# Layer 1 attention: GpSimd's moments between its last fetches, and ScalarE's four normalisations at the end of an iteration

## The chip, the core and the metric

The kernel runs on one core of one Trainium2 chip. The metric is the device time of one execution, in microseconds; the median of the runs shown is compared. TensorE (PE) multiplies and transposes, VectorE (DVE) and ScalarE (ACT) work elementwise, GpSimd (POOL) computes moments and issues the indirect transfers, SyncE (SP) issues the plain ones. Each engine runs its own program in the order in which it is written, and semaphores tie them together.

## The reference, cut to what matters

128 sequences of 64 tokens with 128 channels go through two layers. Each layer is a gated cross attention on a layernorm of x, and then a gated mixture of eight experts. The change lies in the second layer's attention (one head, causal) and in the first steps of its router.

```python
x = x + tanh(g_xattn[0]) * L0_xattn(layernorm(x), ctx, ctx)   # 16 heads
x = x + tanh(g_ffn[0])   * L0_ffn(layernorm(x))               # top 2 of 8 experts
x = x + tanh(g_xattn[1]) * L1_xattn(layernorm(x), ctx, ctx)   # 1 head, causal
x = x + tanh(g_ffn[1])   * L1_ffn(layernorm(x))               # each expert takes its 17 best tokens of a sequence

# L1_ffn
scores = softmax(einsum('bsd,ed->bse', x, router_w))
gate_vals, sel_idx = top_k(swapaxes(scores, 1, 2), 17)
tokens = x[b_idx, sel_idx]
y = gelu(tokens @ w1 + b1) @ w2 + b2
out = zeros_like(x).at[b_idx, sel_idx].add(y * gate_vals)
```

Every layernorm needs mean and variance of each token's 128 channels. Every token's row is in a tile of 128 tokens, so there are 64 tiles, in 16 groups of four.

## The kernel before, in words

Four stages follow each other: layer 0 attention (to about 337 us of the profiled span), layer 0's experts, layer 1 attention (about 584 to 684 us), and layer 1's experts. The stages overlap a little at their edges. No scheduler takes part: each engine's order is that of the Python loops in `scalar_program`, `tensor_program`, `vector_program`, `gpsimd_program` and `sync_program`, and tables of numbers at the top say in which iteration a side task is done.

**Layer 1 attention** is a loop over u from -2 to 16 that all engines write out with the same index. In iteration u:

- PE transposes the normalised tokens of group u+2 (`turn_tokens1`, L640), multiplies the keys' folded projection of group u+2 (`project1`, L936) and the values of group u+1 (`values1`, L943), transposes the shifted scores of group u (`turn1`, L967), computes the scores of group u+1 (L954, L958) and the output of group u (`output1`, L980).
- ACT copies the transposed tokens of group u+2 out of PSUM (L1723), normalises two tiles of group u+3 (`norm1`, L1880), copies the projection (`projected1`, L1900), computes the exponentials of group u (L1910) and normalises the other two tiles of group u+3.
- DVE finds the largest score of group u (L1536), subtracts it (L1540), adds the attention's output of group u-1 to x (L1551, L1554), copies the values of group u+1 with their bias (L1546), and then does side work: `combine(t)` adds layer 0's expert results of a late tile t (two instructions, L1451), `statistics1` and `statistics_router1` take a group's sums (L1124) before its layernorm and before the router.

**From iteration 7 on** (`ROUTE1_FROM`) the router's first call, `route1(0)`, is threaded through the loop. Each engine makes three steps of it in an iteration. Its steps on PE are the transposes of x (L777) and the logits (L809) of groups 0 to 3, on ACT the copies of both (L1723, L1921). DVE waits through eight steps and in the ninth, at the end of iteration 9, multiplies the logits by the inverse standard deviations (L1571). That step waits for the semaphores `s_lg1` (ACT's four copies of logits) and `s_mom2` (GpSimd's moments of 16 tiles). After it come the softmax, a transpose (L1016), and the choice of the 17 best tokens (L1583 to L1586, L1592 to L1595), which ends in iteration 11.

**GpSimd** fetches layer 0's expert results of tiles 48 to 63 in this stage (`get`, two indirect transfers a tile, L2100). A fetch waits until DVE has combined the tile six before it, since six buffers go round. `moments` turns sums into the mean times the inverse deviation and the inverse deviation (eleven or ten small instructions, L2006 to L2018; the power is L2014) for eight tiles. `moments1` serves the attention's `norm1`, `moments_router1` the router.

**SP** stores each finished group of x (L609) and, after the store of group `SPREAD_AT`, spreads the chosen tokens' lists (L587 to L604). DVE's `pick1` of tiles 0 to 3 (L1613, L1127), in iterations 14 and 15, waits for them. `LATER_BY` says how many of the last 16 tiles are combined by the end of iteration u: iteration 7 combines tiles 59 and 60, iteration 8 tiles 61 and 62, iteration 9 tile 63.

After the loop PE gathers the chosen tokens (L1031), ACT copies them (L1941), and the experts of layer 1 begin (L1067, L1077), with GpSimd adding their results to the output (L2182).

Of the kernel before, what the change touches and what calls it, by code (L numbers as in the profile page):

```python
# [23 lines left out]
TG = 4  # L24
NG = NT // TG
# [9 lines left out]
TS = 8  # L35
NSG = NT // TS
NS = 16
# [7 lines left out]
PARTS = ((0, 24), (24, 24), (48, 16))  # L45
# [70 lines left out]
COUNT_AT, SOFTMAX_AT, GATES_AT = 11, 12, 18  # L116


SPREAD_AT = 11
PICKED = {14: (0, 1), 15: (2, 3)}  # L120

LATER_BY = (0, 1, 3, 5, 7, 9, 11, 13, 15, 16)


def later_by(u):
    return LATER_BY[max(0, min(u, len(LATER_BY) - 1))]

# [88 lines left out]
def build(nc, t_in, out):  # L216
    with ExitStack() as ctx:
# [3 lines left out]
        def sem(name):  # L221
            return ctx.enter_context(nc.semaphore(name))
# [154 lines left out]
        def vec(name, n=1):  # L377
# [54 lines left out]
        s_st3, s_mom2, s_ltr1, s_lnTr1, s_lgm1, s_lg1 = [sem(n) for n in (  # L432
            "s_st3", "s_mom2", "s_ltr1", "s_lnTr1", "s_lgm1", "s_lg1")]
# [31 lines left out]
        def sync_program(e):  # L465
# [141 lines left out]
            for g in range(NG):  # L607
                w.wait_ge(s_x3, TG * g + TG)
                e.dma_start(out[:, TG * g:TG * g + TG, :], x_sb[:, TG * g:TG * g + TG, :]).then_inc(s_out, 16)  # L609
                if g == SPREAD_AT:  # L610
                    spread_lists(0)
# [1092 lines left out]
        def scalar_program(e):  # L1704
# [170 lines left out]
            def norm1(g, tiles):  # L1875
                w.wait_ge(s_mom1, g // 2 + 1)
                w.wait_ge(s_lt1, g - 1)
                for t in tiles:
                    n = TG * g + t
                    ins = e.activation(ln_sb[:, g % 2, t, :], x_sb[:, n, :], ACT.Identity, bias=nmr[:, n:n + 1], scale=rstd[:, n:n + 1])  # L1880
                if t == TG - 1:
                    ins.then_inc(s_ln1, 1)
# [13 lines left out]
            def projected1(g):  # L1896
                w.wait_ge(s_sc1, g - 1)
                w.wait_ge(s_g1, g + 1)
                w.wait_ge(s_yb, NBL - NW + 1)
                e.activation(g1[:, g % 2, :], banks[7], ACT.Identity, bias=fold1[:, 3:4]).then_inc(s_ge1, 1)  # L1900

            def tokens1(g):
                w.wait_ge(s_sc1, g - 1)
                w.wait_ge(s_q, NG)
                copy_turned(g % 2, 6, s_lt1, s_lnT1, g)
# [39 lines left out]
            for u in range(-2, NG + 1):  # L1945
                if u + 2 < NG:
                    tokens1(u + 2)
                if 2 <= u + 3 < NG:
                    norm1(u + 3, (0, 1))
                if u >= ROUTE1_FROM:  # L1950
                    next(side, None)
                if u + 2 < NG:
                    projected1(u + 2)
                if u >= ROUTE1_FROM:
                    next(side, None)
                if 0 <= u < NG:
                    exponentials1(u)
                if 2 <= u + 3 < NG:
                    norm1(u + 3, (2, 3))
                if u >= ROUTE1_FROM:  # L1960
                    next(side, None)
                for t in PICKED.get(u - 1, ()):
                    copy_gathered(t, FIRST_BANKS[t % 2])
            for _ in side:
# [28 lines left out]
        def gpsimd_program(e):  # L1993
# [8 lines left out]
            def moments(lo, n, s_in, count, s_done, raised=False):  # L2002
                w.wait_ge(s_in, count)
                me, qe, mo, qo = [stats[:, lo:lo + n, k] for k in (1, 2, 4, 5)]
                a, b, c, d = [ln_tmp[:, k, 0:n] for k in range(4)]
                step.then_inc(e.tensor_tensor(b, me, mo, ALU.subtract))  # L2006
                step.then_inc(e.tensor_tensor(c, qe, qo, ALU.add))
                step.done(e.tensor_tensor(a, me, mo, ALU.add))
                step.then_inc(e.tensor_scalar(b, b, 0.5, None, ALU.mult))
                step.done(e.tensor_scalar(c, c, 1.0 / D, EPS, ALU.mult, ALU.add))  # L2010
                step.done(e.tensor_tensor(b, b, b, ALU.mult))
                step.then_inc(e.tensor_tensor(d, b, c, ALU.add))
                step.done(e.tensor_scalar(a, a, -0.5, None, ALU.mult))
                step.done(e.tensor_tensor(rstd[:, lo:lo + n], d, minus_half[:, 0:n], ALU.pow))  # L2014
                ins = e.tensor_tensor(nmr[:, lo:lo + n], a, rstd[:, lo:lo + n], ALU.mult)
                if raised:
                    step.done(ins)
                    ins = e.tensor_scalar(nmr[:, lo:lo + n], nmr[:, lo:lo + n], 1.0, None, ALU.add)  # L2018
                ins.then_inc(s_done, n // TS or 1)
                made[s_done.num] += n // TS or 1  # L2020
                w.wait_ge(s_done, made[s_done.num])
# [114 lines left out]
            def moments1(lo):  # L2136
                moments(lo, TS, s_st2, lo + TS, s_mom1, raised=True)

            def moments_router1(lo):
                moments(lo, TS, s_st3, lo + TS, s_mom2)  # L2140


            for t in range(PARTS[-1][0]):
# [7 lines left out]
            for t in range(PARTS[-1][0], NT):  # L2151
                get(t)
                if t == PARTS[-1][0] + 1:
                    moments1(PARTS[-1][0] - TS)
            moments1(PARTS[-1][0])
            for lo in range(0, NS, TS):
                moments_router1(lo)
            moments1(NT - TS)
            for lo in range(NS, 2 * NS, TS):
                moments_router1(lo)  # L2160
# [35 lines left out]
        @block.scalar  # L2196
        def _(e):
            scalar_program(e)
# [73 lines left out]
```

## Time and profile before

| | us |
|---|---|
| median of 3 runs | 1008.53 |
| lowest and highest | 1006.76, 1013.9 |
| the profiled execution, its own time | 1011.25 |
| its span in the trace | 1009.4 |
| PE busy | 901.7 (89%) |
| POOL busy | 643.8 (64%) |
| DVE busy | 585.1 (58%) |
| ACT busy | 558.5 (55%) |

The trace covers one execution on the core. The span is the time from its first to its last record; the execution's own time is 1.85 us longer. In the timeline of an engine every row gives the start, the duration, the line with its operation and tiles, and, in brackets, how long the engine had been idle before and what ended that. Busy time of PE includes the time in which its clock is lowered, so the granted clock is read beside it.

### The profile page before, as it was taken

How to read it: one execution, taken by the hardware profiler on the slowest of the kernel's cores; microseconds unless marked ns; L12 is line 12 of the kernel's file. 1: busy time of each engine (PE TensorE's matmuls, PEld its weight loads, DVE VectorE, ACT ScalarE, POOL GpSimd, SP SyncE). 2: the span in 40 equal slices, each digit the busy share in tenths (PEclk: the TensorE clock that was granted, in tenths of full speed). 3: DMA queues.
4: the chain of work that ended last, by engine and by line, in shares of the span. 5: the costliest groups of instructions: out<-in, count | busy, mean ns of one | idle time of the engine just before them, and what ended most of it. 6: DMA issues, size and time to landing. Idle time of an engine off the chain costs nothing.

```text
span 1009.4 us, 25345 instructions
## 1 busy us (share of the span) xinstructions
PE 901.7 (89%) x9084; PEld 747.0 (74%) x9084; DVE 585.1 (58%) x1556; ACT 558.5 (55%) x1337; POOL 643.8 (64%) x795
## 2 busy tenths in 40 slices
PE   5998998898649999999999989778999999999991
PEld 3776776676539989999989966555776766878881
DVE  6887989998755463245526769774535225433320
ACT  2786877687524545444545666436454545454440
POOL 6452454368777757476437777713886658878885
PEclk9999999999959999999999999879999999999996
DMA  9365321133646647665466663150543735665453
GB/s 371 123 194 176 125 82 41 33 117 120 198 140 203 212 150 222 202 208 183 157 203 187 190 234 106 40 145 16 108 46 35 138 24 54 110 77 55 54 55 45
DMA packets 130156, 130.73 MB, mean 130 GB/s; under 512 B 33010, under 2 KB 102770, under 8 KB 129138
## 3 DMA queue, kind: packets, MB, share of 16 engines
q1 hardware_dynamic: 99810, 91.66, 29.0%
q0 software_dynamic: 28928, 29.91, 18.3%
q10 hardware_dynamic: 1296, 7.54, 1.8%
q8 instruction: 76, 1.25, 0.5%
q14 instruction: 46, 0.38, 0.1%
HBM read 53.84 MB, written 49.62 MB: 103 GB/s over the span
## 4 chain that ended last, share of the span: by engine, by line
PE 54%; POOL 13%; issue 11%; DMA 8%; DVE 7%; ACT 4%; SPq 1%; ACTq 0%; POOLq 0%; DVEq 0%
PE psum L888 9%; PE psum L904 9%; PE psum L1067 8%; PE psum L1077 8%; POOL work L2100 4%; POOL xg L2086 3%; PE psum L694 3%; PE psum L681 2%; PE psum L1031 2%; DMA odd<-ln_sb,dest 2%; PE psum L711 2%; POOL odd L2182 2%; DMA out_x<-ln_sb,dest 1%; POOL out_x L2182 1%; DMA work<-yg,place 1%
## 5 line engine op out<-in xcount | busy, mean ns | idle before, releaser
L1872 ACT ACTIVATE hid_sb<-psum,work 128x128 f32<-128x128 f32 (+1 forms) x424 | 145.3, 411 | 149.8 <-PE psum L888 145.7
L2100 POOL DMA_INDIRECT work<-yg,place x128 | 122.1, 954 | 68.6 <-issue 35.7
L888 PE MATMUL psum<-work 128*128 128x128 f32 (+1 forms) x848 | 150.8, 321 | 2.7 <-issue 2.5
L904 PE MATMUL psum<-w_sb,hid_sb 128*128 x1192 | 150.2, 275 | 0.0
L904 PEld LDWEIGHTS psum<-w_sb,hid_sb 128*128 128x128 f32 x1192 | 144.7, 192 | 2.1
L1067 PE MATMUL psum<-work,w_sb 128*128 128x272 f32 (+2 forms) x512 | 132.4, 400 | 5.1 <-ACT ctx_sb L1973 3.1
L2182 POOL DMA_INDIRECT out_x<-ln_sb,dest x68 | 105.9, 1558 | 46.8 <-DVE ln_sb L1668 26.9
L888 PEld LDWEIGHTS psum<-work 128*128 128x128 f32 x848 | 124.8, 193 | 11.6 <-issue 4.4
L1973 ACT ACTIVATE ctx_sb<-psum,w_sb 128x272 f32<-128x272 f32 (+2 forms) x256 | 115.9, 487 | 27.6 <-PE psum L1067 23.9
L1077 PE MATMUL psum<-ctx_sb,w_sb 128*128 128x272 f32 (+2 forms) x512 | 128.1, 392 | 0.0
L2182 POOL DMA_INDIRECT odd<-ln_sb,dest x68 | 105.8, 1556 | 31.9 <-issue 16.5
L2086 POOL DMA_INDIRECT xg<-work,place x104 | 100.5, 966 | 38.8 <-issue 24.1
L1067 PEld LDWEIGHTS psum<-work,w_sb 128*128 128x128 f32 x512 | 92.9, 191 | 32.7 <-ACT ctx_sb L1973 9.0
L2051 POOL TENSOR_SCALAR work<-work,vec_sb 128x512 f32<-128x512 f32 x64 | 43.5, 697 | 102.0 <-ACT work L1735 73.7
L1443 DVE TENSOR_TENSOR yg_sb<-psum,work 128x128 f32<-128x128 f32 (+1 forms) x106 | 36.5, 344 | 122.2 <-PE psum L904 120.2
L1077 PEld LDWEIGHTS psum<-ctx_sb,w_sb 128*128 128x128 f32 x512 | 92.0, 190 | 15.5 <-issue 0.2
L1653 DVE TENSOR_SCALAR work<-psum,b2T_sb 128x272 f32<-128x272 f32 (+6 forms) x96 | 36.0, 403 | 93.2 <-PE psum L1077 93.2
L1941 ACT COPY work<-psum 128x272 f32<-128x272 f32 x64 | 24.8, 387 | 117.8 <-PE psum L1031 117.5
L1208 DVE TENSOR_REDUCE mx<-psum 128x32 f32<-128x2048 f32 x32 | 73.3, 2291 | 21.0 <-PE psum L681 20.5
L1754 ACT ACTIVATE work<-psum 128x512 f32<-128x512 f32 x128 | 70.0, 595 | 22.2 <-PE psum L694 22.1
L1668 DVE TENSOR_TENSOR ln_sb<-psum,slot_sb 128x256 f32<-128x256 f32 (+1 forms) x64 | 28.2, 441 | 88.0 <-PE psum L1088 87.7
L1214 DVE TENSOR_TENSOR w_sb<-psum,mx 128x2048 f32<-128x2048 f32 x32 | 73.0, 2281 | 0.1
(265 smaller groups left out, 1575.7 us busy)
## 6 DMA issues: line engine op xcount, KB each, us to landing
work<-w_sb SPq DMA_DIRECT2D x76, 322.0 KB
work<-xg SPq DMA_DIRECT2D x73, 128.0 KB
yg<-yg_sb SPq DMA_DIRECT2D x73, 128.0 KB
xg<-yg_sb SPq DMA_DIRECT2D x24, 384.0 KB
ctx_sb<-tok SPq DMA_DIRECT2D x8, 1088.0 KB, 6.3
ctxn<-sums_sb SPq DMA_DIRECT2D x64, 64.0 KB, 2.1
out_x<-x_sb SPq DMA_DIRECT2D x16, 256.0 KB, 2.2
odd<-yg_sb SPq DMA_DIRECT2D x10, 384.0 KB
```

What stands on the lines that cost most here:

```text
L888: e.matmul(banks[UP_BANKS[c]][:, 0:cols], w1g(b)[:, c * P:c * P + P], xgT_sb[:, u % 2, at:at + cols], start=True, stop=True).then_inc(s_up, 1)
L904: ins = e.matmul(banks[DOWN_BANKS[b % 2]][:, n * D:n * D + D], hid0[:, b % 2, c, n * P:n * P + P], w2_sb[:, bass.ds(number, 1), c, :].rear ...
L1067: e.matmul(banks[b][:, 0:m * SLOTS], w1_sb[:, ex, c * P:c * P + P], xgT[sg % 2][:, ex, 0:m, :].rearrange("p t s -> p (t s)"), start=True, ...
L1077: ins = e.matmul(banks[3][:, 0:SIZES[sg] * SLOTS], w2_sb[:, ex, c, :], hid[:, ex % 2, c, 0:SIZES[sg], :].rearrange("p t s -> p (t s)"), st ...
L1208: e.tensor_reduce(mx[:, p % 2, :], four_banks, AX_X, ALU.max).then_inc(s_mx, 1)
L1214: e.tensor_tensor(pr[:, i, :, :, :, :].rearrange("p j u h k -> p (j u h) k"), four_banks, mx[:, i, :].unsqueeze(2).to_broadcast([P, 2 * HE ...
L1754: e.activation(dst, banks[B_T[half]], ACT.Exp, scale=SCALE0).then_inc(s_pT, 1)
L1872: e.activation(hid0[:, b % 2, c, 0:cols], banks[UP_BANKS[c]][:, 0:cols], ACT.Gelu, bias=w1g(b)[:, HID + c:HID + c + 1]).then_inc(s_hg, 1)
L1973: e.activation(hid[:, ex % 2, c, 0:m, :].rearrange("p t s -> p (t s)"), banks[(HC * ex + c) % 3][:, 0:m * SLOTS], ACT.Gelu, bias=w1_sb[:, ...
L2086: e.indirect_dma_start(xg_dram[h], at, src, None).then_inc(s_put[i], 16)
L2100: e.indirect_dma_start(dst[:, k, :], None, yg_dram[h], at).then_inc(s_get[i], 16)
L2182: e.indirect_dma_start(sum_rows[n % 2], at, yr[:, n % RESULTS, i, :], None, compute_op=ALU.add, bounds_check=NT * P - 1).then_inc(s_add1[n ...
```

## The change

Five edits are made together. The three tables or constants: `SPREAD_AT` goes from 11 to 10, and `LATER_BY` combines tile 59 in iteration 7, tile 60 in 8, tile 61 in 9, and tiles 62 and 63 in 10. On ACT the two halves of `norm1` become one call for four tiles, after the iteration's third router step. On GpSimd, `moments1` for tiles 48 to 55 (group 12 is the first of them) moves between the fetches of tiles 59 and 60, and the router's moments of tiles 0 to 15 move between the fetches of tiles 61 and 62, as one call for 16 tiles instead of two for eight.

```diff
-SPREAD_AT = 11
+SPREAD_AT = 10
 PICKED = {14: (0, 1), 15: (2, 3)}
-LATER_BY = (0, 1, 3, 5, 7, 9, 11, 13, 15, 16)
+LATER_BY = (0, 1, 3, 5, 7, 9, 11, 12, 13, 14, 16)
...
             for u in range(-2, NG + 1):
                 if u + 2 < NG:
                     tokens1(u + 2)
-                if 2 <= u + 3 < NG:
-                    norm1(u + 3, (0, 1))
                 if u >= ROUTE1_FROM:
                     next(side, None)
...
                 if 0 <= u < NG:
                     exponentials1(u)
-                if 2 <= u + 3 < NG:
-                    norm1(u + 3, (2, 3))
                 if u >= ROUTE1_FROM:
                     next(side, None)
+                if 2 <= u + 3 < NG:
+                    norm1(u + 3, range(TG))
...
-            def moments_router1(lo):
-                moments(lo, TS, s_st3, lo + TS, s_mom2)
+            def moments_router1(lo, n=TS):
+                moments(lo, n, s_st3, lo + n, s_mom2)
...
                 if t == PARTS[-1][0] + 1:
                     moments1(PARTS[-1][0] - TS)
-            moments1(PARTS[-1][0])
-            for lo in range(0, NS, TS):
-                moments_router1(lo)
+                if t == PARTS[-1][0] + 11:
+                    moments1(PARTS[-1][0])
+                if t == PARTS[-1][0] + 13:
+                    moments_router1(0, NS)
             moments1(NT - TS)
```

ACT before, from the token copy of iteration 7 to the second pair of norms of iteration 8 (L1723 copies transposed tokens or, in a router step, transposed x; L1921 copies logits):

```order
L1723 COPY lnT<-psum 128x512
L1880 ACTIVATE ln_sb<-x_sb,nmr,rstd 128x128 x2
L1723 COPY lnT<-psum 128x512
L1900 ACTIVATE work<-psum,fold 128x512
L1921 COPY lg_sb<-psum 128x32
L1910 ACTIVATE work<-psum 128x256
L1880 ACTIVATE ln_sb<-x_sb,nmr,rstd 128x128 x2
L1723 COPY lnT<-psum 128x512 x2
L1880 ACTIVATE ln_sb<-x_sb,nmr,rstd 128x128 x2
L1921 COPY lg_sb<-psum 128x32
L1900 ACTIVATE work<-psum,fold 128x512
L1723 COPY lnT<-psum 128x512
```

ACT in the change, the same two iterations:

```order
L1723 COPY lnT<-psum 128x512 x2
L1900 ACTIVATE work<-psum,fold 128x512
L1921 COPY lg_sb<-psum 128x32
L1910 ACTIVATE work<-psum 128x256
L1723 COPY lnT<-psum 128x512
L1880 ACTIVATE ln_sb<-x_sb,nmr,rstd 128x128 x4
L1723 COPY lnT<-psum 128x512
L1921 COPY lg_sb<-psum 128x32
L1900 ACTIVATE work<-psum,fold 128x512
L1723 COPY lnT<-psum 128x512
L1910 ACTIVATE work<-psum 128x256
L1921 COPY lg_sb<-psum 128x32
```

All four norms now stand behind the exponentials (L1910) and behind a third router step: in iteration 7 the copy of transposed x, in iteration 8 that of the logits.

GpSimd in the change, from the fetches of tiles 60 and 61 (four transfers) on; the file has two lines fewer above, so L2098 is the fetch and L2012 the power:

```order
L2098 DMA work<-yg,place 128x128 x4
L2004 TENSOR_TENSOR work<-stats 128x16
L2005 TENSOR_TENSOR work<-stats 128x16
L2006 TENSOR_TENSOR work<-stats 128x16
L2007 TENSOR_SCALAR work<-work 128x16
L2008 TENSOR_SCALAR work<-work 128x16
L2009 TENSOR_TENSOR work<-work 128x16
L2010 TENSOR_TENSOR work<-work 128x16
L2011 TENSOR_SCALAR work<-work 128x16
L2012 TENSOR_TENSOR rstd<-work,minus_half 128x16
L2013 TENSOR_TENSOR nmr<-work,rstd 128x16
L2098 DMA work<-yg,place 128x128 x4
```

Before, all 28 transfers of the last 14 tiles stood in one run and every moment came behind them. Now the last four transfers wait behind the router's moments.

DVE at the end of iteration 10 (L1546 copies values, L1576 takes the transposed scores):

```order
 L1554 SCALAR_TENSOR_TENSOR x_sb<-psum,sm,x_sb 128x128 x4
 L1546 TENSOR_TENSOR work<-psum,tbo_sb 128x4x128
-L1124 BN_STATS stats<-x_sb 128x6 x4
+L1451 SCALAR_TENSOR_TENSOR x_sb<-work,gate,x_sb 128x128 x4
+L1124 BN_STATS stats<-x_sb 128x6 x8
 L1576 COPY scores_r<-psum 128x128
 L1583 MAX top<-scores_r 128x8
```

Two tiles are combined there that were combined in earlier iterations, and a group's sums are taken that were taken in iteration 9.

## Rows read from the trace of the kernel before

**Rows 1.** Timeline of DVE, end of iteration 9 and beginning of 10.

```profile
637.70 0.69 DVE L1546 TENSOR_TENSOR work<-psum,tbo_sb 128x512 f32<-128x512 f32 x1 [0.43 <-PE psum L943]
638.30 0.73 DVE L1451 SCALAR_TENSOR_TENSOR x_sb<-work,gate,x_sb 128x128 f32<-128x128 f32 x2
639.07 1.65 DVE L1124 BATCH_NORM_STATS2 stats<-x_sb 128x6 f32<-128x128 f32 x8
646.22 0.33 DVE L1571 TENSOR_TENSOR lg_sb<-lg_sb,rstd 128x128 f32<-128x128 f32 x1 [5.50 <-POOL nmr L2015]
...
647.12 0.41 DVE L1536 TENSOR_REDUCE sm<-psum 128x4 f32<-128x256 f32 x1
...
647.90 0.27 DVE L1243 TENSOR_REDUCE red<-lg_sb 128x16 f32<-128x128 f32 x1
```

**Rows 2.** Timeline of POOL: last fetch of tile 63, first router moments.

```profile
632.01 0.94 POOL L2100 DMA_INDIRECT work<-yg,place  x1 [0.30 <-issue]
...
637.72 0.21 POOL L2006 TENSOR_TENSOR work<-stats 128x8 f32<-128x8 f32 x1
```

**Rows 3.** Groups of POOL instructions by shape, power of 16 columns.

```profile
L2014 POOL TENSOR_TENSOR rstd<-work,minus_half 128x16 f32<-128x16 f32 x1 | 3.0, 3014 | 0.1
```

**Rows 4.** Timeline of PE, iteration 3, and the start of iteration 4.

```profile
603.92 0.66 PE L640 MATMUL psum<-ident,ln_sb 128*128 128x128 f32 x4
...
606.16 0.38 PE L967 MATMUL psum<-ident,work 128*128 128x128 f32 x2
...
607.80 0.66 PE L640 MATMUL psum<-ident,ln_sb 128*128 128x128 f32 x4
```

**Rows 5.** Timeline of ACT, iterations -1, 0 and 3.

```profile
590.04 0.87 ACT L1880 ACTIVATE ln_sb<-x_sb,nmr,rstd 128x128 f32<-128x128 f32 x2
...
593.66 1.28 ACT L1910 ACT_TABLE_LOAD   x1
...
605.15 0.88 ACT L1880 ACTIVATE ln_sb<-x_sb,nmr,rstd 128x128 f32<-128x128 f32 x2
605.93 0.67 ACT L1900 ACTIVATE work<-psum,fold 128x512 f32<-128x512 f32 x1
606.58 0.38 ACT L1910 ACTIVATE work<-psum 128x256 f32<-128x256 f32 x1
606.86 0.87 ACT L1880 ACTIVATE ln_sb<-x_sb,nmr,rstd 128x128 f32<-128x128 f32 x2
```

**Rows 6.** Timeline of DVE, values of iteration 3, start of iteration 4.

```profile
606.68 0.68 DVE L1546 TENSOR_TENSOR work<-psum,tbo_sb 128x512 f32<-128x512 f32 x1
...
609.58 0.42 DVE L1536 TENSOR_REDUCE sm<-psum 128x4 f32<-128x256 f32 x1
```

**Rows 7.** Timeline of PE, iterations 7, 8 and 9, with router steps.

```profile
625.38 0.44 PE L967 MATMUL psum<-ident,work 128*128 128x128 f32 x2 [0.16 <-DVE work L1540]
...
628.23 0.66 PE L777 MATMUL psum<-ident,x_sb 128*128 128x128 f32 x4
...
631.72 0.41 PE L967 MATMUL psum<-ident,work 128*128 128x128 f32 x2
...
634.36 1.06 PE L809 MATMUL psum<-wrc,lnT 128*128 128x8 f32 x8
635.27 0.63 PE L640 MATMUL psum<-ident,ln_sb 128*128 128x128 f32 x4
```

**Rows 8.** Timeline of ACT, router copies of iterations 7 and 8.

```profile
628.92 1.08 ACT L1723 COPY lnT<-psum 128x512 f32<-128x512 f32 x2 [0.70 <-PE psum L777]
...
635.46 0.19 ACT L1921 COPY lg_sb<-psum 128x32 f32<-128x32 f32 x1 [0.99 <-PE psum L809]
```

**Rows 9.** Timeline of DVE, start of iteration 11, tile 0 in iteration 14.

```profile
654.73 0.42 DVE L1536 TENSOR_REDUCE sm<-psum 128x4 f32<-128x256 f32 x1
...
672.16 0.36 DVE L1613 TENSOR_SCALAR ctx_sb<-ctx_sb,rowcol_sb 128x272 f32<-128x272 f32 x1 [0.46 <-DMA ctx_sb<-tok]
```

**Rows 10.** One stretch: length, busy PE PEld DVE ACT POOL, clock, DMA share, GB/s.

```profile
648.00:656.00 8.00, 7.04 (x53) 5.06 (x53) 7.13 (x32) 3.31 (x8) 5.83 (x14) 0.63 0.09 34
```

## The prediction

> **What bounds the kernel now.** I read the page's slices first, then the timelines of the five engines from 586 to 700 us, and wrote down, for each iteration u of the loop, three times: T(u), when PE begins the transposes of group u+2 (L640), E(u), when it begins those of the scores of group u (L967), and D(u), when DVE begins with group u (L1536). The reader should see two loops. The first is PE and ACT: a norm ends, PE transposes, ACT copies, exponentials, norms again; it takes 3.88 us (607.80 less 603.92) [rows 4]. The second is DVE alone. Iteration 3 shows 2.90 us from its copy of values to D(4) (609.58 less 606.68) [rows 6], and from there to iteration 9 its timeline lists hardly a wait, so DVE sets the pace there and PE has slack. Then comes the one large hole: in iteration 9 DVE waits 5.50 us for the router's moments, which GpSimd has queued behind its fetches [rows 1, 2]. After it PE runs for a while at a granted clock of 0.63, which is mostly the lower of its levels, 1.2 GHz [rows 10].
>
> **GpSimd's part.** The sums for the router's 16 tiles are complete at D(9). One call for 16 tiles then takes: two calls of eight last from 637.72 to about 646.1, so 4.2 each [rows 1, 2]; the power of 16 columns takes 3.01 [rows 3], and if half of it is added to 4.2 the call takes 5.7 us. Even were it to take two calls' 8.4, this is what must be compared with the time at which DVE wants the result. So the 5.50 us can go completely, if nothing else is late in their place. `moments1` for group 12 moves from behind the fetches to between them: one block of some 4.7 us on POOL that delays the fetches of tiles 60 and on, which wait for nothing else, and `LATER_BY` has moved their combines later. I cost it at nothing; its cover is the later combines.
>
> **ACT's part, first iterations.** Now four norms stand behind the exponentials. Four take 0.78 + 0.87 = 1.65 us (start of a pair to the next instruction, and one pair) [rows 5]. In iteration -1 they begin at 590.04 and PE follows 0.07 later (607.80 after 606.86 + 0.87) [rows 4, 5]: T(0) = 591.76. Before it was 590.98 by the same sum. In iteration 0 the table load began 2.68 after T(0) [rows 5]; without the norm pair ahead I take 2.28, between the 2.68 and 1.9 that a whole pair would leave. T(1) = 591.76 + 2.28 + 1.28 + 0.28 + 1.65 + 0.07 = 597.3. From then on the loop is E(u) = T(u) + 2.24, exponentials 0.42 later, norms 0.28 later, 1.65, 0.07 [rows 4, 5]: **4.66 instead of 3.88**. T(3) = 606.6. DVE's copy of the values follows T by 2.43 (637.70 less 635.27, with its bracket naming PE L943) [rows 1, 7]: 609.05, and D(4) = 609.05 + 2.90 = 611.95, against 609.58. **+2.4 us**. The bounds are 0, if PE's slack hid all of it, and 3.1, four times 0.78. In iterations 4 to 6 DVE's own work sets the pace again and +2.4 stays.
>
> **ACT's part, router iterations.** Here the four norms also stand behind the third router step. E(7) = 625.38 + 2.4 = 627.8. The second router transpose comes 2.85 after it, ACT 0.69 later, the copy lasts 0.54 (half of 1.08) [rows 7, 8]; with norms and 0.07, T(8) = 633.60. DVE copies values at 636.03; with 0.60, one combine 0.77 and four sums 0.83 [rows 1], D(9) = 638.2. In iteration 8 the logits of group 1 stand ahead of L967: E(8) = 633.60 + 2.24 + 0.91 = 636.75. The next logits come 2.64 after it, ACT's copy of them 1.10 later, 0.1, norms, 0.07: T(9) = 642.3, against 635.27 [rows 7, 8]. DVE copies values at 644.7 and has combined and summed at 646.9. ACT's last copy of logits is at T(9) + 4.7 = 647.0 (2.24, transposes and copy 0.6 each, logits 1.1, copy 0.2). So L1571 runs at **647.0, where it ran at 646.22**, and the moments have been ready since 638.2 + 5.7 = 643.9. The removed wait has been spent: PE's values and ACT's logits end last there.
>
> **Iteration 10.** ACT's exponentials and norms follow at 647.0: T(10) = 649.0. ACT copies the tokens (0.69 + 0.54) before it reaches the router's exponentials (0.3), so L1243 runs at 650.6 against 647.90 [rows 1]: +2.7. Then the two combines (2 x 0.77) and four more sums (0.83) that `LATER_BY` put here: D(11) = 654.73 + 5.1 = **659.8** [rows 1, 9].
>
> **What comes back.** The lists are spread after group 10's store instead of 11's, about one iteration sooner, so the 0.46 us for which `pick1(0)` waits goes [rows 9]. And the half clock: in 648 to 656 PE is busy 7.04 us at 0.63; at full clock that is 4.4, so 2.6 less, of which DVE, busy 7.13 of 8.00, covers all but 0.9 [rows 10]. If the stage stays at full clock, something between 0.5 and 3.1 us returns by its end. I take 2.0, since iterations 12 to 15 have little side work on DVE and so follow PE. Combines in iterations 7 and 8 (2 x 0.77 less) are already in the sum. The Trainium skill, "TensorE: Matmul & The Clock Gate", section "HAM oscillation — how this bites in real kernels", says that a wait that recurs lowers the clock again each time; by it nothing comes back, and the sum would be 5.1. The trace has one such place so far, 0.63 behind the 5.50 us wait.
>
> **Sum.** -5.5 (the wait) + 6.3 (values and logits late at L1571, a net of +0.8 there) + 1.9 (router's exponentials) + 2.4 (combines and sums) = +5.1 at D(11), less 2.0, gives **+3.1 us**. The experts' stage after it starts that much later and is otherwise the same on every engine. Against the profiled execution's 1011.25 this is 1014.35; against the median of 1008.53 it is **1011.6**. (The profiled execution lies 2.7 above the median, which is the scatter of the runs.) The change's own bounds are +0.5 (all of 3.1 back, and half of the early 2.4 and of iteration 10's late work hidden) and +5.1.
>
> **Rival 1, faster: the norms are hidden.** PE has slack before DVE's work, and if it absorbs the longer ACT loop, L1571 follows directly on the sums at 640.7 (639.07 + 1.65) and the 5.50 us are won: 1008.5 - 5.5 = 1003.0. For it: DVE had no waits in iterations 4 to 8. Against it: the slack is small. E(4) could have been 607.80 + 2.24 = 610.0 and was not before D(4) + 0.9 = 610.5 (two DVE instructions of 0.42) [rows 4, 6], and the 1.65 us of norms behind each router copy have nothing of PE's beside them. Chance 0.22.
>
> **Rival 2, slower: the lower clock holds.** Place: PE between iterations 10 and 11. E(10) = 649.0 + 2.24 = 651.2, T(11) = 651.2 + 2.42 = 653.7 (0.42, 0.28, 1.65, 0.07), so PE is done with iteration 11's first part at 655.9 and waits for D(11) + 0.9 = 660.7, so it idles 4.8 us. If the clock drops there and stays down to the gathers, an iteration costs at most twice 3.88, 7.8, instead of 4.66, 3.1 more; three or four of the five after it are not covered by DVE, some 10 us: 3.1 + 10 = 13, so 1021 to 1022. It decides if two stretches of 0.5 follow each other without a return. For it: 0.63 after the wait of before. Against: a mean of 0.63 over 8 us means that the clock was back at full within them [rows 10], and PE has work in every iteration. Chance 0.09.
>
> **Rival 3: fetches are late instead.** The last of the four transfers now starts at 643.9 + 0.5 + 3 x 1.25 = 648.2 (0.94 and 0.30 each) [rows 2]. Before, tile 63's combine came 6.3 us after its last transfer began, without a wait (638.30 less 632.01) [rows 1, 2]; that less is enough is not shown. The combines are wanted past 650.6 + 1.9, so at least 4.3 us after. Each us missing is one more on D(11): up to 2 us, 1013.6. The same happens if GpSimd's wait for the router's sums holds it longer, since tiles 62 and 63 are behind it. Chance 0.09.
>
> **Numbers.** Forecast (+0.5 to +5.1) 0.60, rival 1 0.22, rival 2 0.09, rival 3 0.09. About 1%, 10 us, is what a measurement of this kernel tells from no change. Only rival 2 passes it: slower 0.08, faster 0.02, within 1% 0.90. The range reaches to rival 1 and over rival 3, and leaves rival 2 out: 1002.5 to 1016.5. The likeliest case alone is 1009.0 to 1013.6.
>
> **What the changed profile would show.** Right: DVE's L1571 without a wait for POOL, at about 647, with waits for PE L943 in iterations 1 to 3, 8 and 9 (the last about 4 us); L640 at 4.7 us intervals in the first iterations; L640 of group 11 near 642; D(11) near 660; the first gathers (L1031) 2 to 4 us later than before. Wrong: L640 intervals of 3.9, L1571 near 641, or ACT idle waiting for `nmr`. If the combines of tiles 62 and 63 show a wait for a transfer, it is rival 3; if the clock reads 0.5 to 0.7 from 660 to 680, rival 2.

## The result, and the profile after

The changed kernel takes 1019.43 us (median of 14 runs, 1013.94 to 1023.18) where the kernel before takes 1010.0 (median of 14, 1006.76 to 1013.9): ratio 1.0083, 95% interval 1.0067 to 1.01. It is slower by some 8.4 us by the ratio and 9.4 by the medians (the ratios here are not simply quotients of the medians), and above the forecast range. The profiled execution spans 1017.0 us instead of 1009.4. Of these 7.6 us, 1.6 lie ahead of the stage (its first L640 comes at 587.61 instead of 586.02, where the two programs are still the same: scatter of single executions). Nearly all the rest, 5.9 us, is in the stage; behind it the two spans differ by 0.1. Its stretch from that L640 to the experts' first L1067 reads, in the columns of [rows 10], before:

```profile
586.02:684.39 98.37, 81.84 (x850) 59.34 (x850) 76.83 (x278) 54.01 (x123) 57.74 (x108) 0.91 0.42 133
```

and after:

```profile
587.61:691.88 104.27, 80.37 (x849) 58.05 (x849) 77.16 (x278) 55.00 (x123) 56.13 (x98) 0.93 0.40 125
```

5.9 us more, with busy times of DVE and ACT that differ by 1 us at most: the stage waits more. All times "in the stage" below count from this first L640. The removed wait comes first. The timeline of DVE after, end of iteration 9 to iteration 11 [rows 1, 9]:

```profile
638.06 0.69 DVE L1546 TENSOR_TENSOR work<-psum,tbo_sb 128x512 f32<-128x512 f32 x1 [2.51 <-PE psum L943]
...
648.29 0.69 DVE L1546 TENSOR_TENSOR work<-psum,tbo_sb 128x512 f32<-128x512 f32 x1 [5.50 <-PE psum L943]
...
650.68 0.29 DVE L1571 TENSOR_TENSOR lg_sb<-lg_sb,rstd 128x128 f32<-128x128 f32 x1
...
654.09 0.28 DVE L1243 TENSOR_REDUCE red<-lg_sb 128x16 f32<-128x128 f32 x1 [1.68 <-ACT lg_sb L1812]
...
662.79 0.42 DVE L1536 TENSOR_REDUCE sm<-psum 128x4 f32<-128x256 f32 x1
```

The bracket at L1571 that named GpSimd is gone. Ahead of it, at L1546, DVE now waits 5.50 us for PE: the values come late. That the two waits are equally long is chance. GpSimd is done long before, as its timeline shows [rows 2, 3]:

```profile
640.39 0.23 POOL L2004 TENSOR_TENSOR work<-stats 128x16 f32<-128x16 f32 x1 [5.61 <-DVE stats L1124]
...
642.67 2.94 POOL L2012 TENSOR_TENSOR rstd<-work,minus_half 128x16 f32<-128x16 f32 x1
...
645.75 0.22 POOL L2013 TENSOR_TENSOR nmr<-work,rstd 128x16 f32<-128x16 f32 x1
```

The moments are ready at 645.97, 4.7 us before L1571. PE is late because it waits for ACT. The timeline of PE after [rows 4, 7]:

```profile
603.47 0.66 PE L640 MATMUL psum<-ident,ln_sb 128*128 128x128 f32 x4 [0.68 <-ACT ln_sb L1880]
...
608.10 0.66 PE L640 MATMUL psum<-ident,ln_sb 128*128 128x128 f32 x4 [0.68 <-ACT ln_sb L1880]
...
635.61 0.66 PE L640 MATMUL psum<-ident,ln_sb 128*128 128x128 f32 x4 [2.22 <-ACT ln_sb L1880]
...
644.18 1.11 PE L640 MATMUL psum<-ident,ln_sb 128*128 128x128 f32 x4 [1.82 <-ACT ln_sb L1880]
645.08 1.92 PE L936 MATMUL psum<-ctx_sb,w_sb 128*128 128x512 f32 x2
...
648.53 0.38 PE L967 MATMUL psum<-ident,work 128*128 128x128 f32 x2
...
663.74 0.44 PE L967 MATMUL psum<-ident,work 128*128 128x128 f32 x2 [4.02 <-DVE work L1540]
...
669.47 1.91 PE L936 MATMUL psum<-ctx_sb,w_sb 128*128 128x512 f32 x2
```

In the first iterations L640 comes every 4.63 us (608.10 less 603.47; 3.88 before) with a wait for the norms. In iterations 8 and 9 that wait is 2.22 and 1.82 us, and behind the second the instructions themselves are long: L640 takes 1.11 instead of 0.66 us. ACT's timeline says why the norms are late [rows 8]:

```profile
633.43 0.59 ACT L1723 COPY lnT<-psum 128x512 f32<-128x512 f32 x1 [1.46 <-PE psum L777]
633.91 1.65 ACT L1880 ACTIVATE ln_sb<-x_sb,nmr,rstd 128x128 f32<-128x128 f32 x4
...
642.40 0.19 ACT L1921 COPY lg_sb<-psum 128x32 f32<-128x32 f32 x1 [1.75 <-PE psum L809]
642.48 1.65 ACT L1880 ACTIVATE ln_sb<-x_sb,nmr,rstd 128x128 f32<-128x128 f32 x4
```

ACT sits idle for 1.46 and 1.75 us for the router's step, and the norms, whose inputs are there, stand behind it. The clock, in the stretches after with the two waits of PE (642.36 to 644.18, and 659.72 to 663.74):

```profile
640.00:648.00 8.00, 5.95 (x54) 4.51 (x51) 2.46 (x9) 2.97 (x8) 6.14 (x12) 0.79 0.09 34
664.00:672.00 8.00, 5.46 (x47) 3.71 (x45) 7.07 (x32) 3.08 (x7) 3.47 (x10) 0.57 0.14 42
```

Granted 0.79 and 0.57: parts of both stretches at 1.2 GHz. The kernel before has such places too, and [rows 10] is only the first of them; these two follow within its stage:

```profile
656.00:664.00 8.00, 5.41 (x50) 3.99 (x49) 7.00 (x33) 3.19 (x7) 0.00 (x0) 0.79 0.10 36
672.00:680.00 8.00, 5.21 (x33) 3.14 (x26) 4.92 (x18) 1.30 (x4) 0.00 (x0) 0.65 0.85 202
```

Summed over the stage, PE is at 1.2 GHz for about 17 us before and 14 after. The change did not add lowered clock. What differs is where it falls: after, one stretch lies in iteration 9, while DVE waits for PE's values.

### The profile page after: what moved, and what is told of

It is laid out like the page before. It is cut to its first block, busy times and chain, and to the rows that moved or that the text cites. A ratio compares the mean times of both kernels' runs of the same rounds, so it can differ in the third digit from the quotient of the medians.

```text
span 1017.0 us, 25333 instructions
## 1 busy us (share of the span) xinstructions
PE 901.5 (89%) x9084; PEld 746.8 (73%) x9084; DVE 587.0 (58%) x1556; ACT 560.1 (55%) x1337; POOL 641.9 (63%) x785
## 4 chain that ended last, share of the span: by engine, by line
PE 57%; POOL 10%; issue 10%; DVE 7%; DMA 7%; ACT 6%; SPq 1%; ACTq 0%; POOLq 0%; DVEq 0%
PE psum L888 9%; PE psum L904 9%; PE psum L1067 8%; PE psum L1077 8%; PE psum L694 3%; POOL work L2098 3%; POOL xg L2084 3%; PE psum L1031 2%; PE psum L681 2%; ACT ln_sb L1880 2%; PE psum L711 2%; DMA odd<-ln_sb,dest 2%; PE psum L640 1%; POOL out_x L2181 1%; PE psum L936 1%
## 5 line engine op out<-in xcount | busy, mean ns | idle before, releaser
L1872 ACT ACTIVATE hid_sb<-psum,work 128x128 f32<-128x128 f32 (+1 forms) x424 | 145.5, 412 | 149.9 <-PE psum L888 149.9
L2098 POOL DMA_INDIRECT work<-yg,place x128 | 122.4, 956 | 69.4 <-issue 34.5
L1067 PE MATMUL psum<-work,w_sb 128*128 128x272 f32 (+2 forms) x512 | 132.5, 400 | 5.1 <-ACT ctx_sb L1971 3.1
L1067 PEld LDWEIGHTS psum<-work,w_sb 128*128 128x128 f32 x512 | 92.9, 191 | 32.7 <-ACT ctx_sb L1971 9.4
```

The source lines that it names most:

```text
L1067: e.matmul(banks[b][:, 0:m * SLOTS], w1_sb[:, ex, c * P:c * P + P], xgT[sg % 2][:, ex, 0:m, :].rearrange("p t s -> p (t s)"), start=True, ...
L1872: e.activation(hid0[:, b % 2, c, 0:cols], banks[UP_BANKS[c]][:, 0:cols], ACT.Gelu, bias=w1g(b)[:, HID + c:HID + c + 1]).then_inc(s_hg, 1)
L2098: e.indirect_dma_start(dst[:, k, :], None, yg_dram[h], at).then_inc(s_get[i], 16)
```

## The experiments

Theory A: the norms' place behind ACT's third router step costs most, the clock that PE's waits lower adds to it, and GpSimd's part alone gains. Theory B: GpSimd's part, with the tables `SPREAD_AT` and `LATER_BY`, is what costs. Theory C: the four norms in one block cost through the first iterations' loop, whatever their place.

The four chips of these runs differ. On two of them the kernel before takes 1233 us, for a reason that these profiles don't name (see the last section); the same programs were run there and on two chips on which it takes 1010. So ratios to the kernel before on the same chip are compared. The changed kernel itself was not run on a 1233 us chip. Milestones in the stage, from one profile of each kernel on a 1010 us chip (us after the first L640):

```
                      D(4)   T(9)   L1571  D(11)  D(15)  L1067  clock
before                23.56  49.25  60.20  68.71  87.20   98.37  0.91
changed               25.85  56.57  63.07  75.18  94.12  104.27  0.93
changed (e5)          25.85  58.22  64.72  76.84  96.05  105.84  0.92
pairs (e6)            23.57  50.89  55.70  67.82  86.18   95.97  0.95
busy (e7)             25.86  56.58  61.42  73.54  90.72  100.50  0.98
late (e8)             25.85  59.21  66.25  75.50  94.02  104.73  0.92
one late (e13)        23.57  49.26  54.07  66.24  85.25   97.84  0.90
one late, busy (e14)  23.56  50.87  55.68  67.79  86.24   96.03  0.95
four ahead (e15)      25.86  52.57  57.40  69.51  88.86   98.63  0.95
spread 11 (e16)       24.86  50.55  55.36  67.47  85.96   96.41  0.93
```

The last column is the stage's mean granted clock. The two profiles of the changed kernel differ by 1.6 us, so in one profile less than that says nothing. Their timelines show what the 1.6 us are. Behind the same wait of iteration 8, PE in e5 reads:

```profile
635.80 0.66 PE L640 MATMUL psum<-ident,ln_sb 128*128 128x128 f32 x4 [2.22 <-ACT ln_sb L1880]
636.30 1.79 PE L936 MATMUL psum<-ctx_sb,w_sb 128*128 128x512 f32 x2
```

In the other profile the same L936 takes 1.02 us. So the same program with the same wait once kept its clock and once did not; each such stretch ahead of L1571 put 1.65 us on it (61.42 in busy with none, 63.07 with one, 64.72 with two). Pairs and one late, busy lost the same 1.6 us by T(9) to a stretch around T(7), where PE has no wait as long as these.

**Pairs.** The changed kernel with the norms back in two pairs; GpSimd's part and the tables stay.

```diff
+                if 2 <= u + 3 < NG:
+                    norm1(u + 3, (0, 1))
                 if u >= ROUTE1_FROM:
                     next(side, None)
...
+                if 2 <= u + 3 < NG:
+                    norm1(u + 3, (2, 3))
                 if u >= ROUTE1_FROM:
                     next(side, None)
-                if 2 <= u + 3 < NG:
-                    norm1(u + 3, range(TG))
```

> The change with its edit on ScalarE undone: norm1 stands in two pairs again, everything else is as changed. Theory A (the four norms in one place cost more than the whole change's loss, and GpSimd's part with the tables gains): 4 to 7 us faster than before, ratio 0.993 to 0.996, L1571 on DVE near 641 without a wait, first L1067 near 679. Theory B (the loss comes from GpSimd's part: tiles 62 and 63 late and their work on DVE in iteration 10): 4 us or more slower than before, ratio above 1.004, as the changed kernel or nearly. Theory C (a lower clock by chance of placement): anything between, with the halved clock in as many us as in the changed kernel (13.6).

> The change with the norms in two pairs as before. Theory A (the four norms are the price): 4 to 7 us faster than before, ratio 0.993 to 0.996, and 10 us or more faster than the changed kernel; on DVE the product with the inverse deviation comes 54 to 55 us after the stage's first transposes (60.2 before, 63.1 changed). Theory B (GpSimd's part and the combines in iteration 10 are the price): 1.004 or more.

On the 1233 us chip (before 1233.18): 1233.9, ratio 0.9993 (0.9972 to 1.0015). On the 1010 us chip (before 1010.57): **1007.18, 0.9978 (0.9962 to 0.9994)**. GpSimd's part with its tables gains 2 us by itself (3.4 by the medians), of the 5.5 of its wait. That is less than the 4 to 7 us that theory A had said. The timelines of DVE, PE and ACT of this kernel say where the rest went:

```profile
642.28 0.29 DVE L1571 TENSOR_TENSOR lg_sb<-lg_sb,rstd 128x128 f32<-128x128 f32 x1
...
645.69 0.29 DVE L1243 TENSOR_REDUCE red<-lg_sb 128x16 f32<-128x128 f32 x1 [1.68 <-ACT lg_sb L1812]
```

```profile
655.34 0.44 PE L967 MATMUL psum<-ident,work 128*128 128x128 f32 x2 [4.02 <-DVE work L1540]
```

```profile
655.53 0.88 ACT L1880 ACTIVATE ln_sb<-x_sb,nmr,rstd 128x128 f32<-128x128 f32 x2 [5.28 <-POOL nmr L2018]
...
656.88 0.36 ACT L1910 ACTIVATE work<-psum 128x256 f32<-128x256 f32 x1
```

L1571 comes 55.70 into the stage instead of 60.20: 4.5 us won. D(11) comes only 0.9 sooner (67.82 against 68.71): 1.68 of wait for the router's exponentials, and the combines and sums that `LATER_BY` put into iteration 10, take 3.6 back. And in iteration 11 ACT now waits 5.28 us for the moments of group 14, with its own exponentials behind that wait.

**Late.** The kernel before with only the norms moved, as in the change: the complement.

```diff
-                if 2 <= u + 3 < NG:
-                    norm1(u + 3, (0, 1))
...
-                if 2 <= u + 3 < NG:
-                    norm1(u + 3, (2, 3))
                 if u >= ROUTE1_FROM:
                     next(side, None)
+                if 2 <= u + 3 < NG:
+                    norm1(u + 3, range(TG))
```

> The kernel before with the edit on ScalarE alone: four norms at the end of an iteration. Theory A: slower than before by 2 us for the loop and up to 5 more if PE's clock falls behind the longer waits, ratio 1.002 to 1.007; L1571 on DVE at 647 to 650, as late as before although its moments are ready by 646. Theory B: within 1 us of before, since DVE's wait for the moments at 640.7 to 646.2 covers any delay of PE.

> The kernel before with the four norms at the end of an iteration and nothing else. Theory A: 2 to 7 us slower than before, ratio 1.002 to 1.007, the product with the inverse deviation at 63 us or later after the stage's first transposes. Theory B: within 1 us of before.

1237.83, 1.0035 (1.001 to 1.0059), and 1015.05, **1.0044 (1.0026 to 1.0062)**. The norms alone cost 4.5 us, so theory B can't be the whole. Its DVE timeline, end of iteration 9:

```profile
648.27 0.69 DVE L1546 TENSOR_TENSOR work<-psum,tbo_sb 128x512 f32<-128x512 f32 x1 [5.50 <-PE psum L943]
...
651.20 0.28 DVE L1571 TENSOR_TENSOR lg_sb<-lg_sb,rstd 128x128 f32<-128x128 f32 x1
```

No bracket for GpSimd here either, though its moments stand where they stood before: with late norms its end is not the bound, and moving it wins nothing. Its median lies 3.2 us under the changed kernel's on the same chip. The two halves do not add up to the whole: late is 1.0044, pairs 0.9978, the change 1.0079. With late norms the rest of the change is a loss, and the milestones show a candidate for it: from L1571 to D(11) late takes 9.25 us and the changed kernel 12.11, since `LATER_BY` put two combines and four sums there. Those 2.9 us are theory B's share. The two profiled stages differ by 1.1 only (105.84 less 104.73), but late's has 10 us at 1.2 GHz ahead of L1571 and e5's 7; that this is the rest is likely and not shown.

**Four ahead.** The changed kernel with its block of four norms one step earlier, ahead of the third router step.

```diff
+                if 2 <= u + 3 < NG:
+                    norm1(u + 3, range(TG))
                 if u >= ROUTE1_FROM:
                     next(side, None)
-                if 2 <= u + 3 < NG:
-                    norm1(u + 3, range(TG))
```

> The change with the four norms ahead of the third router step instead of behind it (they still stand behind the exponentials). Theory A with the router step as the larger part of the price: 2.4 us stay lost in iterations 0 to 3, D(10) comes near 645 and the kernel ends 1 to 3 us below before, 3 to 4 us or more below the changed one. If the loop in all iterations is the price and not the router step, it stays within 1.5 us of the changed kernel.

> The changed kernel with the four norms ahead of the third router step instead of behind it. Theory A with the router step as the larger part: the 2.3 us of iterations 0 to 3 stay, the product with the inverse deviation comes 58 to 59 us after the stage's first transposes (63.1 to 64.7 changed), ratio to before 0.999 to 1.002. If the loop of the other iterations is the price: 1.006 or more, with that product past 62 us.

> The changed kernel with the four norms ahead of the third router step. If the norms behind the router step are most of the price: PE begins the transposes of iteration 9 at 52 us or earlier after the stage's first (56.6 changed), the product with the inverse deviation comes at 59 to 60 (63.1 to 64.7 changed), no half clock before iteration 10, ratio to before 1.000 to 1.003. If the other iterations' loop is the price, the product comes past 62 and the ratio is 1.006 or more.

On 1233 us chips 1.0029 (1.0 to 1.0058) and 1.0024 (0.999 to 1.0057); on a 1010 us chip (before 1009.81) 1011.13, **1.0000 (0.9981 to 1.0018)**. One step's order is worth some 8 us (1.0083 and, repeated, 1.0079 against 1.0000). I had expected 1 to 3 us below before in the first of these runs; it isn't reached on either kind of chip. ACT and then PE of this kernel, iterations 8 and 9:

```profile
632.04 1.64 ACT L1880 ACTIVATE ln_sb<-x_sb,nmr,rstd 128x128 f32<-128x128 f32 x4
633.61 0.58 ACT L1723 COPY lnT<-psum 128x512 f32<-128x512 f32 x1
```

```profile
633.74 0.66 PE L640 MATMUL psum<-ident,ln_sb 128*128 128x128 f32 x4 [0.16 <-ACT ln_sb L1880]
...
640.36 0.66 PE L640 MATMUL psum<-ident,ln_sb 128*128 128x128 f32 x4
```

The norms fill the time in which ACT waited for the router's matmuls, and PE's waits of 2.22 and 1.82 us shrink to 0.16 and none. L1571 comes 5.67 us sooner than in the changed kernel (57.40 against 63.07): 4.0 by T(9), the rest the clock of iteration 9. This is theory A's part. D(4) is still at 25.86: the longer loop of the first iterations stays, and its 2.3 us are as much as the distance to pairs (1.0000 against 0.9978). Theory C has that part and no more.

**Busy.** The changed kernel, with products that nobody reads in PE's idle time, into banks that the next real product overwrites: 18 before `turn1(11)`, 11 before `output1(11)`, 10 and 8 at the ends of iterations 7 and 8, 9 in iteration 15.

```diff
+BUSY_TURN, BUSY_OUTPUT, BUSY_END = {11: 18, 15: 6}, {11: 11, 15: 3}, {7: 10, 8: 8}
...
+            def keep_busy(bank, n):
+                wait_bank(bank)
+                for _ in range(n):
+                    e.matmul(banks[bank][:, 0:256], ident_b[:], mask_b[:].unsqueeze(1).to_broadcast([P, TG, S]), start=True, stop=True)
...
+                if u in BUSY_TURN:
+                    keep_busy(3, BUSY_TURN[u])
...
+                if u in BUSY_END:
+                    keep_busy(6, BUSY_END[u])
```

> The changed kernel with idle time of PE filled: 10 and 8 additional products of 256 columns (0.2 us each) at the end of iterations 7 and 8, 18 and 6 ahead of the scores' transposes of iterations 11 and 15, 11 and 3 ahead of their outputs. They write PSUM that the next step overwrites; nothing reads them. Theory clock (part of the loss is PE's halved clock in 644 to 648 and 665 to 671): the half clock goes, L640 in iteration 9 takes 0.66 and not 1.11, and it is 2 to 4 us faster than the changed kernel. Rival (the waits themselves are the loss, PE's speed is covered by DVE): no change or up to 1 us slower than the changed kernel.

> The changed kernel with idle time of PE filled by 36 products in iterations 7, 8, 11 and 15, and more ahead of outputs (56 in all). Theory clock: no halved clock between the stage's start and the gathers (13.6 us of it in the changed kernel), T(9) to E(9) 2.8 us and not 4.4, and 2 to 4 us faster than the changed kernel. Rival (DVE's waits cover it): within 1 us of the changed kernel.

On the 1233 us chip 1.004 (1.0013 to 1.0067). Without the changed kernel on such a chip, that tells neither gain nor loss. On the 1010 us chip **1013.28, 1.0024 (1.0003 to 1.0045), where the changed kernel itself takes 1018.22**: 5 us, more than the 2 to 4 expected. A stretch with the wait of iteration 9, and PE's timeline there (L641, L937 and L973 are L640, L936 and L967):

```profile
638.00:646.00 8.00, 6.38 (x67) 5.00 (x63) 3.77 (x12) 3.90 (x10) 6.32 (x12) 1.00 0.10 36
```

```profile
642.00 0.66 PE L641 MATMUL psum<-ident,ln_sb 128*128 128x128 f32 x4 [0.93 <-ACT ln_sb L1892]
642.50 1.02 PE L937 MATMUL psum<-ctx_sb,w_sb 128*128 128x512 f32 x2
...
644.68 0.38 PE L973 MATMUL psum<-ident,work 128*128 128x128 f32 x2
```

Same program, clock 1.00 instead of 0.79: from L640 to L967 it takes 2.68 us instead of 4.35 (648.53 less 644.18), and the two kernels, level at T(9) (56.58, 56.57), are 1.65 apart at L1571. A wait of 2.06 us before `turn1(11)` is left, and the clock still falls there once: 661 to 669 reads 0.86. The kernel before with its own idle time filled was not run, so these 5 us are not a part of the 8 that separate the two kernels: it too has about 17 us at 1.2 GHz to win back.

**The changed kernel again**, on the chip of pairs, late and busy.

> The changed kernel itself, beside the others on one chip. If this chip runs the kernel before at about 1010 us: 1.005 to 1.010 of it, as measured, with DVE waiting 2.5 and 5.5 us for the values in iterations 8 and 9. If it is a chip on which the indirect fetches land late (kernel before at 1233 us): DVE waits for the fetches in iterations 2 to 5 instead, and the ratio is within 0.4% of 1.

1018.22, 1.0079 (1.0054 to 1.0104): the result stands. Rival 3's sign, a combine of tile 62 or 63 that waits for a transfer, is in neither profile: the four L1451 instructions of iteration 10 have no bracket. One combine does wait 0.8 us for a transfer in both, but for an earlier tile, just ahead of the stage's first L640.

**One late.** Pairs everywhere but in iteration 11, where ACT waits for the moments; there all four norms go behind the exponentials, still ahead of the third router step.

```diff
+                if 2 <= u + 3 < NG and u != 11:
+                    norm1(u + 3, (0, 1))
...
+                if 2 <= u + 3 < NG:
+                    norm1(u + 3, range(TG) if u == 11 else (2, 3))
```

> The change with pairs of norms in every iteration but 11, where the four norms of group 14 stand at the end. Theory A (the late norms pay only where a norm would wait for GpSimd's moments of group 14, 5.28 us in e6_pairs, and block the projection and exponentials behind it for 1.1 us): 0.5 to 1.5 us faster than e6_pairs, ratio to before about 0.997. Rival (the wait is covered by DVE): equal to e6_pairs within 0.3 us, the output of iteration 11 as late after DVE's subtraction as there.

> Pairs of norms in every iteration but 11, on a chip that runs the kernel before at about 1010 us. Theory A: 0.5 to 1.5 us faster than e6_pairs had been against before (0.9978), so 0.996 to 0.9975, since the exponentials of iteration 11 no longer stand behind a wait for group 14's moments. Rival: 0.9978 within 0.0005, if DVE's own work covers the 1.1 us.

0.9986 (0.9955 to 1.0018) on a 1233 us chip; on a 1010 us chip 1007.28, **0.9969 (0.995 to 0.9988)**. ACT in iteration 11:

```profile
654.97 0.38 ACT L1910 ACTIVATE work<-psum 128x256 f32<-128x256 f32 x1 [4.90 <-PE psum L967]
655.25 1.64 ACT L1880 ACTIVATE ln_sb<-x_sb,nmr,rstd 128x128 f32<-128x128 f32 x4
```

The exponentials no longer stand behind the norms' wait. Against pairs (0.9978) the gain is under 1 us and the intervals overlap. The profiles point to the rival: in both kernels `output1(11)` begins 4.7 us after D(11) behind a wait for DVE (L1554).

**One late, busy.** The same with the products before `turn1` {11: 17, 15: 6} and `output1` {11: 10, 15: 3}.

> As e9_one_late, with 17 and 6 additional products ahead of the scores' transposes of iterations 11 and 15 and 10 and 3 ahead of their outputs, as in e7_busy. Theory clock: the half clock of 6.8 us after iteration 11 goes and 1.5 to 3 us with it, ratio to before 0.993 to 0.996. Rival (the clock cost 5 us in the changed kernel only because the late norms left PE with no slack): within 0.7 us of e9_one_late.

> The same with PE's idle time of iterations 11 and 15 filled. Theory clock: the 6.8 us of half clock that e6_pairs has after iteration 11 go; 1.5 to 3 us faster than e13_one_late, ratio to before 0.993 to 0.996, 24 to 26 us from DVE's start of iteration 11 to the experts' first product (28.2 in e6_pairs). Rival (the clock cost much only with late norms): within 0.7 us of e13_one_late.

0.9998 (0.9974 to 1.0022); and **1004.05, 0.9948 (0.9927 to 0.9968)**, beside one late's 1007.28 on the same chip. It beats both kernels: 5.8 us under the one before by the medians, some 13 under the changed one. The ratio is as expected, the profile is not. PE's wait in iteration 11 is half filled (L973 is L967), and the output behind it (L986) still runs at the lower clock, 1.14 us instead of 0.67:

```profile
654.68 0.44 PE L973 MATMUL psum<-ident,work 128*128 128x128 f32 x2 [2.15 <-DVE work L1550]
...
658.45 1.14 PE L986 MATMUL psum<-work 64*64 64x129 f32 x16 [0.74 <-DVE x_sb L1564]
```

From D(11) to L1067 it takes 28.24 us, as pairs does without the products (28.15); 24 to 26 was expected. One late takes 31.60. So the 3 us against one late are measured, but the profiles show the clock less lowered than in one late, and no less than in pairs.

**Spread 11.** Pairs with `SPREAD_AT` back at 11.

> e6_pairs with SPREAD_AT at 11 as before. Theory (with GpSimd's part the lists must leave an iteration sooner or DVE waits for the tokens in iteration 14): 1 to 2 us slower than e6_pairs, ratio about 1.000, a wait of 1 us or more of pick1(0) for the tokens. Rival (lists are early enough either way): within 0.4 us of e6_pairs.

> e6_pairs with SPREAD_AT at 11. Theory: DVE waits 1 to 2 us for the tokens in iteration 14 and the kernel is 1 to 2 us slower than e6_pairs, ratio to before 0.999 to 1.000. Rival: within 0.4 us of e6_pairs (0.9978).

1.0036 (1.0006 to 1.0065) on a 1233 us chip; 1008.28, 0.9985 (0.997 to 1.0) on a 1010 us one. The wait for the tokens is back in DVE's timeline:

```profile
670.62 0.36 DVE L1613 TENSOR_SCALAR ctx_sb<-ctx_sb,rowcol_sb 128x272 f32<-128x272 f32 x1 [0.58 <-DMA ctx_sb<-tok]
```

It is shorter than the 1 to 2 us expected. Whether its 0.58 us reach the end, the two ratios (0.9985, 0.9978) don't tell apart.

## Why the prediction failed, step by step

The forecast for the stage was +3.1 us; the two profiles have +5.9 and +7.5. Two terms of the sum were wrong: the +0.8 at L1571, which was +2.9 and +4.5, and the 2.0 given back behind D(11), of which 0.6 and 0.7 came.

- **GpSimd's part** was right: no wait for GpSimd, the moments ready at 58.4 in the stage (forecast 57.9), the power of 16 columns at 2.94 us [rows 3]. That the wait would be spent again before L1571 was right too.
- **ACT's part, first iterations** was right: T(0) at 5.70 in the stage (forecast 5.74), loop 4.63 (4.66), D(4) at 25.85 (25.9). Rival 1, norms hidden in PE's slack, did not happen; its chance of 0.22 was spent on a slack that the prediction had itself found small.
- **ACT's part, router iterations** was right up to the values: T(8) at 48.0 (47.6), T(9) at 56.57 (56.3). There the first step failed. I let PE run from T(9) to the logits at full clock, 4.7 us. In iteration 9 the granted clock was 0.79 in the mean, it took 6.5 us, and L1571 came at 63.07 where I had 61.0; with PE kept busy it came at 61.42. In the second profile iteration 8 ran slow as well, and L1571 came at 64.72.
- **Iteration 10** was right in size: L1571 to D(11) 12.11 us, forecast 12.8. D(11) at 75.18 (73.8); kept busy, 73.54. The sum of +5.1 over before at D(11) is +4.8 with PE kept busy, and the clock puts 1.6 on it, 3.3 in the second profile.
- **What comes back** is the second step that failed. I gave back 2.0 us because the half clock of [rows 10] would go. That was wrong in two ways. The lowered clock of [rows 10] lies ahead of D(11) in the kernel before (at 654.09, 68.1 in the stage, an L943 takes its full-clock 1.05 us again; D(11) is at 68.71), so its going had nothing to give behind D(11). And I wrote that the trace had one such place; it has three, two of them in 656 to 664 and 672 to 680. Behind D(11) the kernel before has some 10 us at 1.2 GHz, and the changed one has as much: PE waits 4.02 us before `turn1(11)`, 664 to 672 reads 0.57, and a later stretch reads 0.82. From D(11) to L1067 the kernel before takes 29.66 us, the changed one 29.09 and 29.00, the busy one 26.96. The line in the Trainium skill that I set beside it ("TensorE: Matmul & The Clock Gate", section "HAM oscillation — how this bites in real kernels": a wait that recurs lowers the clock each time) gave nothing back. It was nearer, with 0.6 us back in the trace, but the trace does not bear out "each time": one and the same wait of 2.22 us was followed by full clock in one profile and by the lower one in the other.
- **Rival 2** had the place right (forecast 4.8 us of idle PE before `turn1(11)`, measured 4.02) and the lower clock behind it. But the clock did not stay down to the gathers (672 to 680 reads 1.00), and since the kernel before has as much lowered time behind D(11), this cost nothing in the comparison. The stretch that did cost was in iteration 9, where I had not looked.
- **Luck**: the +5.1 at D(11) is within 0.3 of the full-clock figure partly because two errors cancel, L1571 0.4 us too early and iteration 10 0.7 too long.
- **The span's remainder** stays open: the medians differ by 9.4 and 7.7 us, the stages by 5.9 and 7.5, and a single profile scatters by 1.6 or more.

What the change bought, then, by ratios: GpSimd's part with its tables, about -2 without late norms; the longer loop of the first iterations, about +2; norms behind the third router step, about +8. In the profiles that last part is 5.7 us at L1571, 4.0 of waits and 1.65 of lowered clock. The parts depend on each other: with late norms, GpSimd's part with its tables costs about 3 instead of gaining.

## What to carry to other kernels

In an engine's in-order list, a step whose inputs are ready must not stand behind one that waits for another engine's side work: here that order alone, one step further down, cost 8 us. Before a wait is moved off one releaser, work out when the next one comes; here PE's values and ACT's logits were due at the same moment. Where a forecast finds idle PE in a loop of small matmuls, it should ask what a stretch of 1.2 GHz behind it would hold up: here 1.65 us each, where DVE waited for PE. It should first read the clock of the whole stage before the change, so that lowered clock which both kernels have is not counted as gain or loss. Products into a bank that is about to be overwritten are a cheap thing to try.

## What the runs showed of the hardware

Filling PE's waits with products of some 0.1 us that nobody reads gained 5 us in the changed kernel (1018.22 to 1013.28) and 3 in one late (1007.28 to 1004.05). The clock fell behind waits of PE of 1.82 to 4.19 us in these traces, but not behind each: a wait of 2.22 us was followed by it in one of two profiles of the same program. And in pairs it fell at T(7), where no such wait stands.

And the same program takes 1010 us on two chips and 1233 on two others. The groups of GpSimd's fetches, after on a 1010 us chip, then pairs on a 1233 us one:

```profile
L2098 POOL DMA_INDIRECT work<-yg,place x128 | 122.4, 956 | 69.4 <-issue 34.5
```

```profile
L2100 POOL DMA_INDIRECT work<-yg,place x128 | 122.1, 954 | 135.3 <-issue 81.6 <-DMA yg<-yg_sb 36.7 <-DVE x_sb L1451 14.6
L1872 ACT ACTIVATE hid_sb<-psum,work 128x128 f32<-128x128 f32 (+1 forms) x424 | 147.7, 412 | 321.5 <-remote 152.3
```

Each fetch takes GpSimd as long; the idle time ahead of them nearly doubles. Those 66 us are at most a part of the 223. ACT's idle time ahead of its activations in layer 0's experts (L1872) grows more, from 149.8 us in the kernel before to 321.5, and for 152.3 of them the profile can't name the releaser ("remote"). In the stage of this change DVE has such waits too, none of them for a fetch by its bracket. So the cause of the slow chips is open. Against the kernel before on the same chip, every variant run there lies between 0.9986 and 1.0040; on the faster chips they lie between 0.9948 and 1.0083.
